# Attention scores of two units in the upper and lower half of TensorE's rows, on odd steps

## The chip, the cores and the metric

The kernel runs on one core of a Trainium2 chip. The metric is device microseconds of the whole program, lower is better. TensorE (PE in the profile) multiplies, VectorE (DVE), ScalarE (ACT) and GpSimd (POOL) work on rows of data, and SyncE (SP) issues most of the transfers. TensorE first loads a stationary operand (PEld) and then streams a moving one past it into PSUM.

## The reference, cut to what matters

Two layers, each an attention and then a mixture of eight experts, over 32 batches of 128 positions with 256 features. The change touches the attentions alone, which have 16 heads of 16 features:

```
q, k, v = layernorm(x) @ Wq, ctx @ Wk, ctx @ Wv    # layer 0 with biases
scores  = einsum('bhqd,bhkd->bhqk', q, k) / 4       # layer 1: minus the causal and the key mask
out     = softmax(scores) @ v                       # 16 heads x 16 features
x       = x + tanh(g) * out                         # layer 0 has W_O in front
```

## The kernel before

**Units.** A unit is four heads of one batch, and there are `NU` = 128 units in each layer (L = 0, 1). Unit i belongs to batch i // 4, and the four units of a batch take heads 0 to 3, 4 to 7, 8 to 11 and 12 to 15. The 256 features lie as two blocks of 128 rows (`m`), so a block holds the heads of two units: the even unit's four heads are rows 0 to 63 and the odd unit's are rows 64 to 127 (`z`). The scores of a unit are one matrix product of the queries (stationary, 128 features x 128 positions) with `KX` (moving, 128 features x 4 heads x 128 keys), in which each head's keys stand in that head's 16 rows and the rest is zero. Each operand is split in a rounded high part and a low rest, and `three` (lines 407 to 411) adds high x high, high x low and low x high. Layer 1 adds the mask with a fourth product (line 488).

**Steps.** Every engine runs through the same list of steps s = -8 to 147, each in its own written order, and they meet at semaphores. Unit i passes so: TensorE makes its scores in step i - 4, into one of three PSUM banks (`SB_[i % 3]`); VectorE takes the row extremes in step i - 3 (line 1094); ScalarE takes the exponentials in step i - 2 (line 698), which frees the bank; TensorE transposes them in step i (line 470), ScalarE copies the transposed weights out (line 705), and TensorE multiplies them with the values in step i + 2 (line 553), each head in 32 columns of the array. When a batch's four units are summed up, ScalarE copies the sums to `OS` (line 691) and TensorE turns them in step 4b + 6 (line 495); VectorE normalises them in the next step (lines 1098 and 1104). The turned weights and sums take turns in two banks (`PTB`).

**Work of a group.** A group is four batches, 16 steps. `grp(s, k)` is true at step k modulo 16. Spread over the 16 steps are the projections for a later group: turned layer norm at steps 6 and 7 (`X0`), queries at 8 and 9 (`Q0`), keys at 0 and 2 (`K0`), values at 10 and 11 (`V0`), and for the router turned rows at 13 and 14 (line 526), logits at 15 (line 534) and ranks at 2 (lines 540 and 541). In layer 0 there is an output projection for each batch too (lines 511 and 517). In layer 0 all these share one PSUM bank (`BK`), and a use waits until the one before it was read (`bank_free`). After a key projection ScalarE takes the high part (line 649 or 651), VectorE the low part (877 or 879, in `dve_rests` of the next step), and SyncE copies a batch's keys into `KX` with eight transfers (`sp_keys`, line 1444).

**Order in a step before.** TensorE: weights of unit s turned, scores of unit s + 4, sums turned, projections, router work, values of unit s - 2. VectorE: extremes of unit s + 3, sums normalised, `dve_rests`, then the rest. ScalarE: sums, exponentials of unit s + 2, turned weights of unit s, then the rest.

Of the kernel before, what the change touches and what calls it, by code (L numbers as in the profile page):

```python
# [11 lines left out]
ALU = mybir.AluOpType  # L12
AX = mybir.AxisListType
# [5 lines left out]
G = 4  # L19
# [106 lines left out]
NU = 4 * B  # L126
FIRST, LAST = -8, 148
X0, Q0, K0, V0 = (6, 7), (8, 9), (0, 2), (10, 11)
# [8 lines left out]
def bat(s, k):  # L137
    b, m = divmod(s - k, 4)
    return b if m == 0 and 0 <= b < B else None


def program(nc, A):
    ctx = ExitStack()
    with ctx:
# [300 lines left out]

        def pe_first(e, w, L):

            if L == 0:
                w.wait_ge(*s_kz[0, 0])
                for n in range(WARM):  # L450
                    e.matmul(PTB[1][:, :], KXR[:, 0:128], KXR[:, 0:512], start=True, stop=True)
            for m in range(2):
                pe_key(e, w, L, 0, m)
            for h in range(2):
                pe_value(e, w, L, 0, h)
            for t in range(2):
                pe_turn(e, w, L, 0, t)
            for m in range(2):
                w.wait_ge(*v_k[L, 0, m])
                pe_query(e, w, L, 0, m)  # L460

        def pe_attention(e, w, L):
            pe_first(e, w, L)
            for s in range(FIRST, LAST):
# [7 lines left out]
                if 0 <= s + 4 < NU:  # L472
                    i = s + 4
                    b, m, z = i // 4, (i // 2) % 2, i % 2
                    g, j, bank = b // G, b % G, SB_[i % 3]
                    w.wait_ge(*v_q[L, g, 1])
                    if i < 2:
                        w.wait_ge(*a_v[L, 0, i])
                    w.wait_ge(*d_k[b % 2][L, b, 7])
                    if i >= 3:  # L480
                        w.wait_ge(*a_p[L, i - 3])
                    js = slice(j * 128, j * 128 + 128)
                    kh, kl = (KX[:, b % 2, p, m, 4 * z:4 * z + 4, :].rearrange("p h k -> p (h k)") for p in range(2))
                    ins = three(e, bank[:, :], (QR[:, g % 2, 0, m, js], QR[:, g % 2, 1, m, js]), (kh, kl), True, L == 0)
                    if L == 1:
                        w.wait_ge(*v_mk[g])
                        w.wait_ge(*s_ir[0])
                        ins = e.matmul(bank[:, :], IR[:, :], MK[:, g % 2, j:j + 1, :].to_broadcast([128, 4, 128]), start=False, stop=True)  # L488
                    ins.then_inc(*m_s(L, i))
                if (b := bat(s, 6)) is not None:  # L490
                    bank = pt_place["o", b]
                    w.wait_ge(*a_o[L, b])
                    turn_free(w, L, "o", b)
                    for n in range(4):
                        ins = e.transpose(bank[:, n * 128:(n + 1) * 128], OS[:, n * 128:(n + 1) * 128], ident)  # L495
                    ins.then_inc(*m_o(L, b))
# [45 lines left out]
                if 0 <= s - 2 < NU:  # L542
# [12 lines left out]
                    ins.then_inc(*m_av(L, i))  # L555

# [528 lines left out]

        def dve_attention(e, w, L):
            dve_first(e, w, L)
            for s in range(FIRST, LAST):
                if 0 <= s + 3 < NU:
                    i = s + 3  # L1090
                    w.wait_ge(*m_s[L, i])
                    if i >= 4:
                        w.wait_ge(*a_p[L, i - 4])
                    e.tensor_reduce(mx[:, i % 4], SB_[i % 3][:, :].rearrange("p (h k) -> p h k", h=4), AX.X, ALU.min).then_inc(*v_mx(L, i))  # L1094
# [14 lines left out]
                dve_rests(e, w, L, s - 1)  # L1109
                for j in range(G):  # L1110
                    if L == 1 and (g := grp(s, -3 + j)) is not None:
                        dve_add_rows(e, w, g * G + j)
# [509 lines left out]
```

## Time and profile before

| | before |
|---|---|
| three runs | 1713.99, 1715.84 and 1717.71 us, median 1715.84 |
| the profiled execution | 1715.62 us, its span 1713.8 us |
| busy: TensorE, weight loads | 1595.4 us, 1406.1 us |
| busy: VectorE, ScalarE, GpSimd | 1199.4, 1233.1, 827.5 us |
| attention of layer 0, steady part | about 60 to 370 us of the span |
| attention of layer 1, steady part | about 940 to 1250 us |

The experts take most of what is left, and the change doesn't touch them. Busy shares are averages over stages, so the steady part of each attention is read by itself. A matmul's duration includes its way through the array: what one costs in a stream is read from the distance of one start to the next, which the chain of waits shows.

### The profile page before, as it was taken

The page shows a single profiled execution, that of the slowest core. Times are in us where ns is not written, and L with a number is a line of the kernel's source. Part 1 is how long each engine was busy: PE and PEld are TensorE (multiplying, and loading weights), DVE is VectorE, ACT ScalarE, POOL GpSimd, SP SyncE. Part 2 cuts the span into 40 slices and gives each one's busy share as a digit, 9 for nine tenths or more (in the row PEclk, how much of TensorE's full clock was granted, in tenths as well). Part 3 has the DMA queues.
Part 4 walks back from the last instruction along what each step waited for, and adds up shares of the span by engine and source line. Part 5 has one row for each costly group of instructions (what it writes and reads, how often), then busy time and mean ns, then how long its engine had stood idle before and what let it go on. Part 6 is the DMA issues. An engine that isn't in the chain of part 4 may idle for free.

```text
span 1713.8 us, 37210 instructions
## 1 busy us (share of the span) xinstructions
PE 1595.4 (93%) x12792; PEld 1406.1 (82%) x12792; DVE 1199.4 (70%) x2843; ACT 1233.1 (72%) x2859; POOL 827.5 (48%) x888
## 2 busy tenths in 40 slices
PE   6999999996899999999995999999994899999996
PEld 4777777774899999999994776776773899999996
DVE  4666777756577777777775778888866666666663
ACT  3887877771688888888872877777782577777774
POOL 3124433434365565656553113333323477777775
PEclk8999999996899999999997999999996999999998
DMA  3222222133877777788762223332231688887883
GB/s 108 50 51 74 72 73 75 51 87 87 246 237 229 227 231 226 229 227 232 225 191 72 76 82 104 98 95 72 90 92 65 204 236 227 225 241 222 229 230 98
DMA packets 208989, 256.57 MB, mean 150 GB/s; under 512 B 29555, under 2 KB 156788, under 8 KB 208800
## 3 DMA queue, kind: packets, MB, share of 16 engines
q1 hardware_dynamic: 186048, 218.22, 43.9%
q0 software_dynamic: 21120, 34.39, 7.8%
q8 instruction: 102, 1.67, 0.4%
q10 hardware_dynamic: 1632, 1.58, 0.3%
q14 instruction: 87, 0.71, 0.1%
HBM read 194.54 MB, written 45.74 MB: 140 GB/s over the span
## 4 chain that ended last, share of the span: by engine, by line
PE 76%; DVE 12%; issue 3%; POOL 3%; DMA 2%; ACT 2%; SPq 1%; POOLq 0%; DVEq 0%; ACTq 0%
PE ps L409 20%; PE ps L411 19%; PE ps L410 19%; PE ps L470 6%; PE ps L553 4%; PE ps L564 2%; DVE mx L1094 2%; POOL xs_scr L1345 1%; PE ps L534 1%; SPq L1444 1%; PE ps L495 1%; PE ps L488 1%; PE ps L526 1%; DVE X L1017 1%; PE ps L424 1%
## 5 line engine op out<-in xcount | busy, mean ns | idle before, releaser
L1217 POOL TENSOR_TENSOR KXR<-U,KXR 128x1024 fp32r<-128x1024 f32 (+1 forms) x156 | 355.4, 2278 | 278.4 <-ACT KXR L750 258.9
L409 PE MATMUL ps<-QR,KXR 128*128 128x256 f32 x1248 | 361.9, 290 | 4.2 <-DVE QR L1221 4.2
L411 PE MATMUL ps<-QR,KXR 128*128 128x256 f32 x1248 | 355.6, 285 | 0.0
L410 PE MATMUL ps<-QR,KXR 128*128 128x256 f32 x1248 | 355.4, 285 | 0.0
L750 ACT ACTIVATE KXR<-U 128x1024 fp32r<-128x1024 f32 (+1 forms) x312 | 287.4, 946 | 75.5 <-PE ps L411 50.4
L698 ACT ACTIVATE U<-ps,mx 128x128 f32<-128x128 f32 x1024 | 294.9, 391 | 26.3 <-DVE mx L1094 26.0
L409 PEld LDWEIGHTS ps<-QR,KXR 128*128 128x128 f32 x1248 | 241.8, 194 | 5.7 <-DVE QR L1221 5.3
L410 PEld LDWEIGHTS ps<-QR,KXR 128*128 128x128 f32 x1248 | 241.8, 194 | 0.0
L411 PEld LDWEIGHTS ps<-QR,KXR 128*128 128x128 f32 x1248 | 241.4, 193 | 0.0
L1094 DVE TENSOR_REDUCE mx<-ps 128x4 f32<-128x512 f32 x256 | 174.9, 685 | 87.2 <-PE ps L411 38.3
L1217 DVE TENSOR_TENSOR KXR<-U,KXR 128x1024 fp32r<-128x1024 f32 (+1 forms) x156 | 176.3, 1168 | 25.7 <-ACT KXR L750 25.5
L1345 POOL DMA_INDIRECT xs_scr<-XR,PI x112 | 109.6, 979 | 142.9 <-DVE PI L1005 113.8
L470 PE MATMUL ps<-cst,U 128*128 128x128 f32 x1024 | 168.4, 287 | 2.7 <-DVE U L1104 2.2
L705 ACT ACTIVATE U<-ps 128x512 f32<-128x512 f32 x256 | 161.8, 632 | 10.8 <-PE ps L470 10.1
L776 ACT ACTIVATE U<-ps,b1s 128x256 f32<-128x256 f32 x312 | 130.1, 471 | 32.5 <-PE ps L411 32.5
L470 PEld LDWEIGHTS ps<-cst,U 128*128 128x128 f32 x1024 | 108.4, 141 | 54.0 <-issue 41.6
L1248 DVE TENSOR_TENSOR PTR<-U,PTR 128x512 fp32r<-128x512 f32 x80 | 100.8, 1295 | 63.2 <-ACT PTR L787 63.2
L409 PE MATMUL ps<-KXR,PTR 128*128 128x256 f32 x480 | 136.3, 284 | 2.4 <-ACT U L765 1.5
L1248 DVE TENSOR_TENSOR WR<-U,WR 128x512 fp32r<-128x512 f32 x76 | 98.0, 1326 | 56.7 <-ACT WR L787 56.7
L410 PE MATMUL ps<-KXR,PTR 128*128 128x256 f32 x480 | 136.0, 283 | 0.0
L411 PE MATMUL ps<-KXR,PTR 128*128 128x256 f32 x480 | 136.0, 283 | 0.0
L409 PE MATMUL ps<-KXR,QR 128*128 128x512 f32 x256 | 122.4, 478 | 14.6 <-ACT U L698 11.5
(204 smaller groups left out, 4042.3 us busy)
## 6 DMA issues: line engine op xcount, KB each, us to landing
U<-in_wpack SPq DMA_DIRECT2D x234, 512.0 KB, 5.0
U<-in_wpack SPq DMA_DIRECT2D x78, 256.0 KB, 4.7
KXR<-U SPq DMA_DIRECT2D x512, 32.0 KB
U<-xs_scr SPq DMA_DIRECT2D x39, 258.0 KB, 4.5
U<-xs_scr SPq DMA_DIRECT2D x39, 257.0 KB, 4.7
U<-in_ctx_t SPq DMA_DIRECT2D x16, 512.0 KB, 5.4
U<-ys_scr SPq DMA_DIRECT2D x32, 256.0 KB, 3.3
XR<-in_L_ffn_b SPq DMA_DIRECT2D x39, 128.0 KB, 4.1
```

What stands on the lines that cost most here:

```text
L409: e.matmul(o, wh, xh, start=first, stop=False)
L410: e.matmul(o, wh, xl, start=False, stop=False)
L411: return e.matmul(o, wl, xh, start=False, stop=done)
L470: ins = e.transpose(bank[:, h * 128:(h + 1) * 128], PB[:, i % 3, h], ident)
L698: ins = e.activation(PB[:, i % 3, h], SB_[i % 3][:, h * 128:(h + 1) * 128], ACT.Exp, bias=mx[:, i % 4, h:h + 1], scale=-1.0)
L705: e.activation(PT[:, i % 3].rearrange("p h k -> p (h k)"), pt_place["p", i][:, :], ACT.Copy).then_inc(*a_pt(L, i))
L750: e.activation(w_cols(L, WH, n), w_raw(L, n), ACT.Copy).then_inc(*a_w[n](L, i))
L776: ins = e.activation(HB[:, r, f], HBK[q][:, z * 256:z * 256 + 256], ACT.Relu, bias=b1s[:, r, f:f + 1])
L1094: e.tensor_reduce(mx[:, i % 4], SB_[i % 3][:, :].rearrange("p (h k) -> p h k", h=4), AX.X, ALU.min).then_inc(*v_mx(L, i))
L1217: e.tensor_tensor(w_cols(L, WL, n), w_raw(L, n), hi, ALU.subtract).then_inc(*l_w[n](L, i))
L1248: ins = e.tensor_tensor(low[:, 2 * q:2 * q + 2], HB[:, i % 2, 2 * q:2 * q + 2], high[:, 2 * q:2 * q + 2], ALU.subtract)
L1345: e.indirect_dma_start(xs_d[L], bass.IndirectOffsetOnAxis(ap=PI[:, g % 2, z, j:j + 1], axis=0), xr(g)[:, z, j, 0:ROWS[L]], None).then_inc( ...
```

## The change

It has four parts.

1. Scores are made on odd steps alone, for units s + 3 and s + 4 together (`pe_scores`). Each of the six products takes 64 of the 128 rows: the even unit's lower half, the odd unit's upper half, in turn, into two banks. In layer 1 the two mask products follow, over all rows.
2. VectorE takes the extremes of unit s + 3 as before on even steps (first in the step), and on odd steps behind `dve_rests` (`dve_least`).
3. TensorE turns the sums at the end of step 4b + 6, behind the values product, and not before the projections.
4. The second key projection of a group moves from step 2 to step 1.

```diff
--- before.py
+++ after.py
@@ -125,7 +125,7 @@
 PARTS = [Part(g, 0, G) for g in range(NG - 1)] + [Part(NG - 1, 0, G - 1), Part(NG - 1, G - 1, G)]
 NU = 4 * B
 FIRST, LAST = -8, 148
-X0, Q0, K0, V0 = (6, 7), (8, 9), (0, 2), (10, 11)
+X0, Q0, K0, V0 = (6, 7), (8, 9), (0, 1), (10, 11)
 
 
 def grp(s, k):
@@ -443,6 +443,31 @@
                                 (WR[:, 2, 0, t], WR[:, 2, 1, t]), t == 0, t == 1)
             ins.then_inc(*m_v(L, g, h))
 
+        def pe_scores(e, w, L, i):
+
+            b, m = i // 4, (i // 2) % 2
+            g, js, banks = b // G, slice(b % G * 128, b % G * 128 + 128), (SB_[i % 3], SB_[(i + 1) % 3])
+            w.wait_ge(*v_q[L, g, 1])
+            if i == 0:
+                for n in range(2):
+                    w.wait_ge(*a_v[L, 0, n])
+            w.wait_ge(*d_k[b % 2][L, b, 7])
+            for n in range(2):
+                if i + n >= 3:
+                    w.wait_ge(*a_p[L, i + n - 3])
+            for q, k in ((0, 0), (0, 1), (1, 0)):
+                for z, bank in enumerate(banks):
+                    hs = slice(64 * z, 64 * z + 64)
+                    ins = e.matmul(bank[:, :], QR[hs, g % 2, q, m, js], KX[hs, b % 2, k, m, 4 * z:4 * z + 4, :].rearrange("p h k -> p (h k)"),
+                                   start=(q, k) == (0, 0), stop=L == 0 and q == 1)
+                    if L == 0 and q == 1:
+                        ins.then_inc(*m_s(L, i + z))
+            if L == 1:
+                w.wait_ge(*v_mk[g])
+                w.wait_ge(*s_ir[0])
+                for z, bank in enumerate(banks):
+                    e.matmul(bank[:, :], IR[:, :], MK[:, g % 2, b % G:b % G + 1, :].to_broadcast([128, 4, 128]), start=False, stop=True).then_inc(*m_s(L, i + z))
+
         def pe_first(e, w, L):
 
             if L == 0:
@@ -469,31 +494,8 @@
                     for h in range(4):
                         ins = e.transpose(bank[:, h * 128:(h + 1) * 128], PB[:, i % 3, h], ident)
                     ins.then_inc(*m_t(L, i))
-                if 0 <= s + 4 < NU:
-                    i = s + 4
-                    b, m, z = i // 4, (i // 2) % 2, i % 2
-                    g, j, bank = b // G, b % G, SB_[i % 3]
-                    w.wait_ge(*v_q[L, g, 1])
-                    if i < 2:
-                        w.wait_ge(*a_v[L, 0, i])
-                    w.wait_ge(*d_k[b % 2][L, b, 7])
-                    if i >= 3:
-                        w.wait_ge(*a_p[L, i - 3])
-                    js = slice(j * 128, j * 128 + 128)
-                    kh, kl = (KX[:, b % 2, p, m, 4 * z:4 * z + 4, :].rearrange("p h k -> p (h k)") for p in range(2))
-                    ins = three(e, bank[:, :], (QR[:, g % 2, 0, m, js], QR[:, g % 2, 1, m, js]), (kh, kl), True, L == 0)
-                    if L == 1:
-                        w.wait_ge(*v_mk[g])
-                        w.wait_ge(*s_ir[0])
-                        ins = e.matmul(bank[:, :], IR[:, :], MK[:, g % 2, j:j + 1, :].to_broadcast([128, 4, 128]), start=False, stop=True)
-                    ins.then_inc(*m_s(L, i))
-                if (b := bat(s, 6)) is not None:
-                    bank = pt_place["o", b]
-                    w.wait_ge(*a_o[L, b])
-                    turn_free(w, L, "o", b)
-                    for n in range(4):
-                        ins = e.transpose(bank[:, n * 128:(n + 1) * 128], OS[:, n * 128:(n + 1) * 128], ident)
-                    ins.then_inc(*m_o(L, b))
+                if s % 2 and 0 <= s + 3 < NU:
+                    pe_scores(e, w, L, s + 3)
                 for name, at, project in (("xt", X0, pe_turn), ("q", Q0, pe_query), ("k", K0, pe_key), ("v", V0, pe_value)):
                     for n in range(2):
                         if (g := grp(s, at[n])) is not None:
@@ -553,6 +555,13 @@
                         ins = e.matmul(OB[32 * h:32 * h + 32, (i % 4) * 128:(i % 4) * 128 + 128], VA[:, v, j % 2, hh * 17:hh * 17 + 32],
                                        PT[:, i % 3, h], start=True, stop=True)
                     ins.then_inc(*m_av(L, i))
+                if (b := bat(s, 6)) is not None:
+                    bank = pt_place["o", b]
+                    w.wait_ge(*a_o[L, b])
+                    turn_free(w, L, "o", b)
+                    for n in range(4):
+                        ins = e.transpose(bank[:, n * 128:(n + 1) * 128], OS[:, n * 128:(n + 1) * 128], ident)
+                    ins.then_inc(*m_o(L, b))
 
         def pe_turn_x(e, w, L, i):
             bank = XB[i % 2]
@@ -1083,15 +1092,17 @@
                 e.tensor_scalar(IR[:, :], ident, NEG_L, None, ALU.mult).then_inc(*s_ir(0))
             e.memset(CR[:, 0], 0.0).then_inc(*v_c.up())
 
+        def dve_least(e, w, L, i):
+            w.wait_ge(*m_s[L, i])
+            if i >= 4:
+                w.wait_ge(*a_p[L, i - 4])
+            e.tensor_reduce(mx[:, i % 4], SB_[i % 3][:, :].rearrange("p (h k) -> p h k", h=4), AX.X, ALU.min).then_inc(*v_mx(L, i))
+
         def dve_attention(e, w, L):
             dve_first(e, w, L)
             for s in range(FIRST, LAST):
-                if 0 <= s + 3 < NU:
-                    i = s + 3
-                    w.wait_ge(*m_s[L, i])
-                    if i >= 4:
-                        w.wait_ge(*a_p[L, i - 4])
-                    e.tensor_reduce(mx[:, i % 4], SB_[i % 3][:, :].rearrange("p (h k) -> p h k", h=4), AX.X, ALU.min).then_inc(*v_mx(L, i))
+                if s % 2 == 0 and 0 <= s + 3 < NU:
+                    dve_least(e, w, L, s + 3)
                 if (b := bat(s, 7)) is not None:
                     w.wait_ge(*m_o[L, b])
                     o = pt_place["o", b][:, :].rearrange("p (h d) -> p h d", d=32)
@@ -1107,6 +1118,8 @@
                         w.wait_ge(*v_on[1, b])
                         e.scalar_tensor_tensor(X[:, b], ON[:, b % 2], th[:, 1:2], X[:, b], ALU.mult, ALU.add).then_inc(*v_xup(1, b))
                 dve_rests(e, w, L, s - 1)
+                if s % 2 and 0 <= s + 3 < NU:
+                    dve_least(e, w, L, s + 3)
                 for j in range(G):
                     if L == 1 and (g := grp(s, -3 + j)) is not None:
                         dve_add_rows(e, w, g * G + j)
```

## Rows read from the trace of the kernel before

**Rows 1.** The windows view, steady part of each attention: busy us of each engine.

```profile
core 0: us, PE busy (x) PEld busy (x) DVE busy (x) ACT busy (x) POOL busy (x), PEclk, DMA share, GB/s
60.00:370.00 310.00, 305.10 (x2587) 235.19 (x2585) 214.36 (x654) 252.10 (x709) 111.69 (x239) 1.00 0.25 65
940.00:1250.00 310.00, 297.35 (x2342) 220.53 (x2341) 252.02 (x727) 231.82 (x661) 93.93 (x220) 1.00 0.31 88
```

**Rows 2.** The chain of waits in layer 0: start us, us, what.

```profile
188.26 0.44 PE ps L424 x4
188.70 0.35 PE ps L553 x8
189.05 0.59 PE ps L470 x4
189.64 0.23 PE ps L409
189.87 0.24 PE ps L410
190.11 0.23 PE ps L411
...
208.33 0.12 PE ps L409
...
211.12 1.68 PE ps L534 x16
```

**Rows 3.** The timeline of layer 0: start us, us, what, idle before and its cause.

```profile
199.93 0.48 PE L409 MATMUL ps<-KXR,QR 128*128 128x512 f32 x1
200.01 0.19 PEld L410 LDWEIGHTS ps<-KXR,QR 128*128 128x128 f32 x1
...
202.59 0.42 PEld L470 LDWEIGHTS ps<-cst,U 128*128 128x128 f32 x4 [0.20 <-issue]
...
204.09 0.16 PEld L553 LDWEIGHTS ps<-U,VA 128*32 128x32 f32 x8 [0.17 <-issue]
```

**Rows 4.** The windows view, one group of 16 steps of layer 0.

```profile
174.40:219.60 45.20, 44.22 (x375) 34.33 (x374) 32.18 (x103) 36.28 (x102) 18.18 (x39) 1.00 0.27 71
```

**Rows 5.** The windows view, one group of 16 steps of layer 1.

```profile
1133.60:1180.30 46.70, 44.39 (x357) 33.06 (x356) 38.78 (x122) 34.35 (x98) 15.85 (x37) 1.00 0.35 97
```

**Rows 6.** Groups of instructions in layer 0: busy us, mean ns, idle before, releaser.

```profile
L698 ACT ACTIVATE U<-ps,mx 128x128 f32<-128x128 f32 x512 | 147.3, 391 | 4.4 <-DVE mx L1094 4.4
L1094 DVE TENSOR_REDUCE mx<-ps 128x4 f32<-128x512 f32 x128 | 87.5, 687 | 48.5 <-PE ps L411 38.3 <-ACT U L698 9.5
...
L705 ACT ACTIVATE U<-ps 128x512 f32<-128x512 f32 x128 | 80.4, 628 | 9.3 <-PE ps L470 8.8
...
L691 ACT ACTIVATE OS<-ps 128x512 f32<-128x512 f32 x32 | 19.3, 605 | 2.7 <-PE ps L553 1.4
```

**Rows 7.** The windows view, slices of 10 us, layer 0.

```profile
220.00:230.00 10.00, 9.02 (x77) 6.50 (x77) 9.12 (x35) 7.25 (x22) 4.63 (x15) 1.00 0.11 24
...
250.00:260.00 10.00, 10.00 (x88) 8.35 (x87) 6.26 (x21) 9.55 (x25) 3.06 (x2) 1.00 0.13 28
...
400.00:410.00 10.00, 5.75 (x23) 4.54 (x22) 6.42 (x44) 2.64 (x7) 2.34 (x6) 0.50 0.10 35
```

**Rows 8.** The windows view, slices of 10 us, layer 1.

```profile
1080.00:1090.00 10.00, 9.55 (x79) 6.81 (x78) 9.17 (x48) 5.96 (x19) 3.11 (x13) 1.00 0.09 19
1090.00:1100.00 10.00, 8.13 (x57) 5.85 (x58) 9.54 (x26) 7.86 (x23) 5.89 (x6) 1.00 0.29 87
```

**Rows 9.** Who waited for whom, TensorE, layer 0: us, times, longest us.

```profile
PE ps L540 <- DVE U L877: 4.9, 5, 1.0
```

**Rows 10.** Who waited for whom, VectorE, layer 0.

```profile
DVE mx L1094 <- PE ps L411: 33.2, 51, 1.5
```

**Rows 11.** The chain of waits in layer 1.

```profile
1022.51 0.23 PE ps L411
1022.74 0.24 PE ps L488
1023.00 0.69 DVE mx L1094
1023.70 0.18 DVE rec L1098
1023.89 0.44 DVE U L1104
1024.35 0.48 DVE X L1108
1024.84 2.59 DVE X L1017
```

**Rows 12.** The timeline of SyncE's queue, layer 0.

```profile
188.34 5.09 SPq L1444 DMA_DIRECT2D KXR<-U  x8
```

## The prediction

> **What bounds the kernel now.** I read the windows of the two steady attentions first. In layer 0 TensorE is busy 305 of 310 us, ScalarE 252 and VectorE 214; in layer 1 it is 297, 232 and 252, all at a granted clock of 1.00 [rows 1]. The chain of waits says the same: in layer 0 it stays on TensorE for tens of microseconds. A step without extra work is 0.35 us for the values product, 0.59 for the turned weights and 3 x 0.233 = 0.70 for the scores, together 1.64 us [rows 2]. ScalarE isn't far behind. Per unit it spends 147.3 / 128 = 1.15 us on exponentials and 80.4 / 128 = 0.63 on the copy, 1.78 in all, which is more than the bare step of TensorE [rows 6]. The units add up to less than TensorE's total only because TensorE has the projections too: a group of 16 steps in layer 0 takes 45.2 us, with TensorE busy 44.2, ScalarE 36.3 and VectorE 32.2 [rows 4]. Inside a group the bound changes: in one slice of 10 us ScalarE is busy 9.55, in another VectorE is busy 9.12 and TensorE idles 0.98 [rows 7]. In layer 1 a group takes 46.7 us with VectorE busy 38.8 [rows 5], for two slices in a row it is at 9.2 and 9.5 while TensorE idles up to 1.9 [rows 8], and the chain passes through it there [rows 11].
>
> **What the change saves on TensorE.** Before, a pair of units costs 6 x 0.233 = 1.40 us of scores [rows 2]. Each product streams 512 columns and keeps the full array, though half of its rows are multiplied with zeros. After, there are still six products of 512 columns, but neighbours sit in different rows. The trace has no such pair, so I bound it. Above: they run one after the other, 1.40 us. Below: the two halves run at once, 3 x 0.233 = 0.70. In between stands the load of the stationary operand, which each product has for itself: sixteen products of 8 columns take 1.68 us, so 0.105 us for a load of 128 columns [rows 2]. Six loads one after another, with the last stream behind them, are 5 x 0.105 + 0.233 = 0.76 us. Do products in different parts of the array overlap at all? The values product does this in columns: eight instructions of 128 columns in 0.35 us, 0.044 each [rows 2], where 128 columns at the rate of the scores (0.233 / 4) would be 0.058 each. That speaks for overlap, though it is weak evidence for rows. I take 0.76, a saving of 0.64 us a pair.
>
> **What it costs on TensorE.** The turned weights take 0.59 us behind the values product, but the same four transposes (lines 424 and 495) take 0.44 behind full products, and the first load behind a change between 32 columns and the full array starts 0.20 or 0.17 us late with nothing to wait for [rows 2, 3]. So a change in how the array is divided costs about 0.15 us. The new scores bring one change on the way in. On the way out there is another one if full-array work follows; with the values product next, that change was there already. Of the eight odd steps of a group in layer 0, six have such work behind the scores (1, 7, 9, 11, 13, 15): 8 + 6 = 14 changes, 2.1 us. In layer 1 the mask product always follows: 16 changes, 2.4 us. From both sides: a change into halves may cost nothing, or 0.20 plus a load, 0.30. The Trainium skill (TensorEngine Tiling (Array Packing), Key Properties) says that changing the tiling mode drains TensorE, while moving to another tile of the same mode does not. The rows agree where they can, with 0.15 us for columns; by the rule the price is there for rows as well, and the sum is the one used here.
>
> Net, a group saves 8 x 0.64 - 2.1 = 3.0 us in layer 0 and 8 x 0.64 - 2.4 = 2.7 in layer 1. If all of it lay on the path, 8 groups each would give 24 + 22 = 46 us.
>
> **How much of it is on the path.** In layer 0 a pair of bare steps is bound by ScalarE already: 2 x 1.78 = 3.56 us, and the copy of sums (19.3 / 32 = 0.60 a batch) comes on top, against TensorE's 3.3 us [rows 2, 6]. Steps 3 to 5 and 12 therefore give nothing back, and in steps 0 to 2 VectorE is nearly full [rows 7]. The projections of steps 6 to 11 and the router's work of 13 and 15 are TensorE's. I count two thirds: 8 x 3.0 x 2/3 = 16 us. In layer 1 about 20 of 46.7 us of a group are VectorE's [rows 5, 8], and the change takes nothing from it; I count half: 8 x 2.7 / 2 = 11 us.
>
> **The key projection.** In layer 0 the rank product (line 540) shares its bank with the key projection and waited for the low part of the keys of the same step, which VectorE makes one step later: 5 waits, 4.9 us [rows 9]. With the projection in step 1, VectorE makes that part in step 2, so this wait goes. What is late next is VectorE itself, full in that slice [rows 7]. I count 3 us. The other side: the second key projection now waits for the low part of the first, one step apart instead of two. Queued behind it on TensorE are the values product of that step and the next turned weights, and ScalarE's copy waits for those. Between the two projections lie 0.35 + 0.59 + 0.91 = 1.85 us of TensorE work; the read-out takes one pass of ScalarE and one of VectorE at about 0.7 each (the extremes of 128 x 512 take 0.687 [rows 6]), so it is just hidden. If not, it costs up to 0.5 us a group, 4 us. In layer 1 there are two banks, so nothing changes.
>
> **The moved pieces.** The scores of the even unit come a step later, and with them its extremes, which stand behind `dve_rests`. The cover is the time until ScalarE wants them in the next step. Now VectorE waits in each odd step for TensorE's scores of that same step, with the statistics and the router's small operations queued behind, and ScalarE waits for those extremes. VectorE's wait at this place is 33.2 us in 51 times already [rows 10], and idle time there has cost nothing. The sums are turned 4 x 0.11 = 0.44 us as before, later in the step by the values product and the extra work (up to 0.35 + 0.7 us); normalising them must be done two transposes later. Between lie 0.59 + 0.91 + 0.35 us, against 0.18 + 0.44 for lines 1098 and 1104 [rows 11]: hidden, nothing. The keys' eight transfers wait for the same odd unit's scores, made in the same step as before, and are issued in 5.1 us [rows 12], and their reader comes one step later, so SyncE's queue has more room. GpSimd's queue isn't touched.
>
> **Sum.** 16 + 11 + 3 = 30 us. The profiled execution took 1715.6 us with a span of 1713.8, 1.8 us around it, and the median is 1715.8, so the two agree: 1715.8 - 30 = 1686 us. With only this case in view, its own range is 1664 (all 46 us and the 4.9 of the wait) to 1704 (0.30 us for each change, which adds 30 x 8 x 0.15 = 36 us on TensorE, of which half counts, 18).
>
> **Rivals.**
>
> A. The halves don't overlap. A pair keeps 1.40 us, and the changes are pure cost: 8 x (2.1 + 2.4) = 36 us. TensorE is the bound, so nearly all of it counts: 36 - 3 = 33, 1749 us. For it: no row shows overlap in rows. Against it: the 0.044 us of the values product [rows 2].
>
> B. A load waits for the stream that still runs in its own half. Each half then goes load, stream, load, stream, 3 x (0.105 + 0.233) = 1.01 us, with the other half 0.1 behind: 1.12 a pair. It saves 8 x 0.28 = 2.2 us a group against 2.1 to 2.4 for the changes, so the time is 1713 to 1717. Against it: the load of line 410 starts at 200.01, while the stream of line 409 over the same rows runs from 199.93 for 0.48 us [rows 3]. The Trainium skill (TensorE: Matmul & The Clock Gate, Part 3) says that a load overlaps a running matmul only when the row group differs. This row of the profile does not agree, and that keeps the chance small.
>
> C. A loop through three engines takes the place of TensorE. The pair of scores at step s needs the exponentials of unit s + 1; then come the extremes of s + 3, its exponentials, and the next pair. That is 0.15 + 0.76 + 0.69 + 1.15 with three handovers of 0.1, 3.1 us (3.3 with the mask), under ScalarE's 3.56. It is the bound once 0.5 us of queueing is added: sums to normalise and rests stand before the extremes, the last copy and a projection's read-out before the exponentials. It loses against before when it costs 30 / 128 = 0.24 us a pair above the forecast. At 0.5 us a pair it costs 64 - 30 = 34 us more than before, 1750; I put the case at 1720 to 1755, its middle at 1735. For it: three banks give only one unit of slack when two are filled at once. Against it: in steps with projections ScalarE has slack.
>
> D. ScalarE and VectorE hide all of it, so only the rank wait shows: 1713 us. For it: ScalarE's 9.55 and VectorE's 9.12 [rows 7]. Against it: in layer 0 TensorE is the chain nearly everywhere.
>
> E. The changes cost little and the rest follows: 8 x 2 x 8 x 0.64 = 82 us at the most, two thirds of it 55: about 1655.
>
> A fall of the granted clock would be visible at once: in a slice with TensorE at 5.8 of 10 us it was 0.50, 1.2 GHz, and with 8.1 busy it stayed 1.00, 2.4 GHz [rows 7, 8]. After the change TensorE is still over 8, so I give that no case.
>
> **How the numbers follow.** Chances: forecast 0.58, A 0.10, B 0.05, C 0.13, D 0.06, E 0.08. Within 0.2% (3.4 us, about what a measurement of this kernel can tell from no change) lie B and D: 0.08, with a bit of each on the fast side. Faster is forecast and E and that bit, 0.69; slower A and C, 0.23. To hold 8 in 10 the range takes half of E, the forecast, B, D and most of C: 1658 to 1738.
>
> **What would show it.** Right: in the chain the six products of a pair together take about 0.76 us, the first load of them starts 0.15 to 0.2 us late, a group of layer 0 takes about 43 us and one of layer 1 about 45.3, the wait of line 540 is gone. Wrong: 0.23 us between starts of neighbours (A), 0.37 us between passes (B), or waits of the scores or the turned weights for ScalarE, and of ScalarE for the extremes, that grow by more than 0.24 us a pair (C).

## The result, and the profile after

The changed kernel takes 1758.05 us in the median of four runs (1752.97 to 1762.94), against 1715.93 before: a ratio of 1.0245 (95% interval 1.0207 to 1.0284), 42 us slower where 30 us faster was forecast. The profiled execution took 1754.1 us, with a span of 1752.3.

The loss lies in the two attentions. The windows view from the first to the last exponential of each layer, first before, then after (span of the window, then busy us of TensorE, its loads, VectorE, ScalarE and GpSimd, then the granted clock):

```profile
29.40:377.70 348.30, 333.79 (x2785) 255.24 (x2784) 234.23 (x699) 277.22 (x783) 120.67 (x266) 0.99 0.26 70
940.60:1291.20 350.60, 334.88 (x2674) 247.48 (x2672) 278.15 (x821) 264.64 (x759) 104.71 (x243) 1.00 0.31 89
```

```profile
29.30:401.10 371.80, 326.72 (x2785) 229.87 (x2786) 233.29 (x699) 275.71 (x783) 120.62 (x266) 0.95 0.24 65
961.50:1329.30 367.80, 328.31 (x2673) 219.01 (x2674) 276.15 (x821) 264.85 (x759) 105.98 (x243) 0.97 0.30 85
```

23.5 us are lost in layer 0 and 17.2 in layer 1. TensorE's work did get less (busy 7 us less in each layer, although its clock is lower). Its idle time grew from 15 to 45 us in layer 0 and from 16 to 40 in layer 1. VectorE and ScalarE do what they did.

TensorE's own terms came out at the forecast size. The chain of waits of the changed kernel, layer 0, which answers to [rows 2]:

```profile
213.91 0.90 PE ps L461 x6
214.81 0.59 PE ps L528 x4
215.40 0.36 PE ps L555 x8
215.75 0.58 PE ps L495 x4
```

And the timeline of its loads, which answers to [rows 3]:

```profile
213.84 0.54 PEld L461 LDWEIGHTS ps<-KXR,QR 64*128 64x128 f32 x6 [0.17 <-issue]
214.74 0.42 PEld L528 LDWEIGHTS ps<-cst,XR 128*128 128x128 f32 x4 [0.36 <-issue]
```

Six products of 64 rows take 0.90 us with the change on the way in (0.76 + 0.15 = 0.91 was forecast), and the four transposes behind them 0.59 in place of 0.44, the change on the way out. So the halves do run at once. The timeline of the same six products, at three moments within it, shows how:

```profile
213.84 0.51 PE L461 MATMUL ps<-KXR,QR 64*128 64x512 f32 x2
214.17 0.40 PE L461 MATMUL ps<-KXR,QR 64*128 64x512 f32 x2
214.40 0.41 PE L461 MATMUL ps<-KXR,QR 64*128 64x512 f32 x2
```

Two products, one in each half, start together, three times. The starts lie 0.33 and 0.23 us apart, and 0.23 is what one full product takes [rows 2]. The prediction had the six loads one after another and so came to 0.76; what runs is three passes of 0.23 us, 0.70, with about 0.2 us on the way in. The sum is the same, its parts are not.

What came on top are waits. Who waited for whom, TensorE and then VectorE, layer 0 of the changed kernel, which answer to [rows 9, 10]:

```profile
PE ps L424 <- DVE U L1047: 16.3, 6, 3.1
PE ps L542 <- DVE U L886: 4.4, 5, 0.9
PE ps L409 <- DVE QR L876: 4.4, 7, 0.6
PE ps L409 <- DVE PTR L870: 3.2, 6, 0.6
```

```profile
DVE rec L1109 <- PE ps L563: 61.8, 29, 3.4
DVE mx L1099 <- PE ps L461: 12.5, 33, 1.0
```

ScalarE waited for the extremes too, before and then after:

```profile
ACT U L698 <- DVE mx L1094: 2.5, 1, 2.5
```

```profile
ACT U L707 <- DVE mx L1099: 16.9, 20, 1.1
```

About once a group TensorE stands before the turned layer norm (line 424), up to 3.1 us, because VectorE's norm (line 1047, 1038 before) is late. The rank product (542) waits as it did. The projections now wait about 0.6 us each time for the read-out of the shared bank (rests 870 and 876). VectorE waits 61.8 us for the sums, where before it waited once, 2.2 us, and less for scores. And the granted clock falls behind the long wait. Windows, two slices of 10 us and a part of the second one, right behind the wait of 3.1 us that ends at 191.46:

```profile
180.00:190.00 10.00, 7.47 (x76) 4.93 (x74) 8.25 (x33) 7.59 (x24) 3.55 (x14) 1.00 0.12 25
190.00:200.00 10.00, 8.02 (x54) 6.04 (x55) 5.89 (x14) 5.87 (x17) 7.98 (x9) 0.83 0.51 159
192.00:195.00 3.00, 3.00 (x20) 2.39 (x20) 0.00 (x0) 1.86 (x6) 2.53 (x3) 0.50 0.78 282
```

In the kernel before all 62 slices of 10 us from 60 to 370 us and from 980 to 1290 us are at 1.00; in the changed kernel eleven of them are at 0.83 to 0.85, and two more at 0.98 and 0.99.

A group of layer 0 takes 48.8 us (181.53 to 230.31, from one rank product to the next) in place of 45.2 [rows 4]; in layer 1 three groups in a row take 48.5 to 50.0 us in place of 46.9. How VectorE's full stretch got longer can be read from its timeline, from the first key rest (line 877, then 886) to the second pair of norms. Before:

```profile
214.48 0.69 DVE L1094 TENSOR_REDUCE mx<-ps 128x4 f32<-128x512 f32 x1
...
216.56 0.75 DVE L877 SCALAR_TENSOR_TENSOR U<-ps,bqk,U 128x512 fp32r<-128x512 f32 x1 [1.39 <-ACT U L649]
...
229.24 0.73 DVE L1038 TENSOR_SCALAR U<-X,mv,rs 128x256 f32<-128x256 f32 x2
```

After:

```profile
224.90 0.75 DVE L886 SCALAR_TENSOR_TENSOR U<-ps,bqk,U 128x512 fp32r<-128x512 f32 x1 [1.52 <-ACT U L658]
...
226.22 0.69 DVE L1099 TENSOR_REDUCE mx<-ps 128x4 f32<-128x512 f32 x1 [0.25 <-PE ps L461]
...
231.90 0.26 DVE L1109 RECIPROCAL rec<-ps 128x16 f32<-128x16 f32 x1 [1.18 <-PE ps L563]
...
239.38 0.72 DVE L1047 TENSOR_SCALAR U<-X,mv,rs 128x256 f32<-128x256 f32 x2
```

12.7 us became 14.5. Before, one reduction ran ahead of the key rest, in time that was idle otherwise (1.39 us were still idle behind it); now its scores don't exist yet at that point, it stands inside the stretch (0.69 + 0.25 us), and 1.18 us go in waiting for the sums. TensorE meanwhile has less to do between rank product and layer norm, so it arrives early and stands.

### The profile page after: what moved, and what is told of

Read it like the earlier page. It is cut to its first block, busy times and chain, and to the rows that moved or that the text cites. A ratio compares the mean times of both kernels' runs of the same rounds, so it can differ in the third digit from the quotient of the medians.

```text
span 1752.3 us, 37272 instructions
## 1 busy us (share of the span) xinstructions
PE 1578.5 (90%) x12792; PEld 1348.8 (77%) x12792; DVE 1196.1 (68%) x2843; ACT 1232.3 (70%) x2859; POOL 828.3 (47%) x888
## 3 DMA queue, kind: packets, MB, share of 16 engines
q10 hardware_dynamic: 1632, 1.58, 0.3%
## 4 chain that ended last, share of the span: by engine, by line
PE 67%; DVE 15%; issue 6%; POOL 4%; DMA 3%; ACT 3%; SPq 1%; POOLq 0%; DVEq 0%; ACTq 0%
PE ps L409 17%; PE ps L411 16%; PE ps L410 16%; PE ps L461 4%; PE ps L495 4%; DVE mx L1099 3%; PE ps L555 2%; POOL xs_scr L1358 2%; PE ps L573 2%; PE ps L563 2%; DMA U<-xs_scr 1%; PE ps L469 1%; PE ps L536 1%; DVE U L1047 1%; DVE PTR L870 1%
## 5 line engine op out<-in xcount | busy, mean ns | idle before, releaser
L495 PEld LDWEIGHTS ps<-cst,U 128*128 128x128 f32 x1024 | 114.0, 144 | 55.7 <-issue 39.5
L461 PE MATMUL ps<-KXR,QR 64*128 64x512 f32 x768 | 127.1, 436 | 10.8 <-ACT U L707 7.8
```

The lines of the kernel that those rows point to most:

```text
L461: ins = e.matmul(bank[:, :], QR[hs, g % 2, q, m, js], KX[hs, b % 2, k, m, 4 * z:4 * z + 4, :].rearrange("p h k -> p (h k)"), start=(q, k) ...
L495: ins = e.transpose(bank[:, h * 128:(h + 1) * 128], PB[:, i % 3, h], ident)
```

## The experiments

Two theories stood at the start. **T**: the sums, turned late, block VectorE at the head of its queue, and all else follows from that. **P**: pairing the scores takes away cover, whatever the sums do. Others were formed on the way.

Eighteen runs were made in five sets, each set on a chip of its own. The chips are of two kinds: on two of them the kernel before takes 1716 to 1717 us, as in the result above, and on three it takes 1760 to 1764 (called the faster and the slower kind below). Ratios are to the kernel before in the same set, and differences in us are taken within one set, or between sets on chips of one kind where it says so. Windows of a layer come from one profiled execution each.

**First set (before: 1763 us, slower kind).** The times expected here were written for a chip on which the kernel before takes 1716 us, so each is read by its distance from the kernel before. What is undone, in short:

```diff
 # e1: the sums turned before the projections, as before
-                if (b := bat(s, 6)) is not None:      # behind the values product
+                if (b := bat(s, 6)) is not None:      # ahead of the projections
 # e3: all score products over full rows
-  QR[hs, g % 2, q, m, js], KX[hs, b % 2, k, m, ...]
+  QR[:, g % 2, q, m, js],  KX[:, b % 2, k, m, ...]
 # e4: the kernel before, sums turned behind the values product, and
-X0, Q0, K0, V0 = (6, 7), (8, 9), (0, 2), (10, 11)
+X0, Q0, K0, V0 = (6, 7), (8, 9), (0, 1), (10, 11)
 # e5: e1, and K0 back to (0, 2)
```

> The changed kernel with one thing undone: the sums are turned before the projections again, as in the kernel before. Theory T (the late turn blocks VectorE at the head of its queue, 61.8 us of its waiting in layer 0, and that makes the layer norm and all behind it late): about 30 to 45 us come back, 1700 to 1725 us, VectorE's wait for the sums falls below 15 us and line 424 waits less than 5 us in layer 0. Theory P (pairing the scores on odd steps takes the cover from the read-outs of the shared bank and from VectorE's work, whatever the sums do): at most 10 us come back, 1745 to 1758 us.

Measured: 1784.5 us, 1.0134 (1.0108 to 1.0161), 21.6 us above before: between the two theories.

> The changed kernel with each of the six score products over all 128 rows, one after another; order and placement as changed. It tells what the halves themselves are worth. If TensorE were still the bound everywhere, a pair would cost 1.40 us in place of 0.76 and save two changes of 0.15 to 0.2 us: 0.3 us a pair, 128 pairs, 35 to 40 us slower than the changed kernel, 1790 to 1800 us. If waits on VectorE and ScalarE are the bound (both theories), about half of it: 1770 to 1780 us.

Measured: 1813.4 us, 1.0289 (1.0260 to 1.0319), 50.5 us above before, less than either case expected. The changed kernel isn't in this set; the fourth set has both.

> The kernel before with two parts of the change alone: the sums turned at the end of the step, and the second key projection in step 1 (the late turn needs it). Theory T: slower by 20 to 40 us than before, 1736 to 1756 us, with VectorE waiting 30 us or more in layer 0 for the sums. Theory P: within 5 us of before.

Measured: 1767.8 us, 1.0032 (1.0012 to 1.0052), 4.8 us above before as P has it, though VectorE does wait 41 us for the sums in layer 0.

> The changed kernel with the turn of the sums and the key projection where they stood before: pairs of scores in halves of the rows and the placement of the extremes alone. Theory T: faster than before, 1690 to 1710 us. Theory P: still slower than before, 1740 to 1758 us.

Measured: 1793.4 us, 1.0173 (1.0139 to 1.0206), 30.4 us above before, as P has it.

Against the 1.0245 of the changed kernel, e1 looked like a gain of 19 us and so like T; the fourth set takes that back. Within this set P holds: with the old turn and the old key projection the paired order is still slower than before (e5). And pairing is dear by itself: e3 and e4 both have full rows, the late turn and the key projection in step 1, and differ in the pairing with its placement of the extremes (which is free when the scores aren't paired, e12). It costs 1813.4 - 1767.8 = 45.7 us. Moving the key projection is worth 8.9 us (e5 against e1). With that, the late turn isn't free either: e4 has both and is 4.8 us slower than before, so by an estimate the late turn costs 12 to 14 us in the old order (4.8 and the 7.4 of e6 or the 8.9).

**Second set (before: 1717 us, faster kind).** The fill goes ahead of the wait for the layer norm, into the bank that is overwritten next:

```diff
 # e7
+            if g and t == 0:
+                for n in range(10):
+                    e.matmul(bank[:, :], WR[:, 0, 0, 0, 0:128], WR[:, 0, 0]..., start=True, stop=True)
             w.wait_ge(*v_ln1[L, g])
 # e8
-X0, Q0, K0, V0 = (6, 7), (8, 9), (0, 1), (10, 11)
+X0, Q0, K0, V0 = (7, 8), (9, 10), (0, 1), (11, 12)
 # e6: the kernel before with K0 = (0, 1)
```

> The changed kernel, unaltered, to have its ratio and its trace on the chip that the other runs of this set share. Both theories: ratio to before 1.02 to 1.03.

Measured: 1764.4 us, 1.0296 (1.0270 to 1.0322).

> The kernel before with the second key projection in step 1 in place of step 2, nothing else. By the prediction 3 us faster (the wait of 4.9 us for the rank product goes); by the rival the projection's new wait for the shared bank costs up to 4 us. Ratio 0.998 to 1.002.

Measured: 1709.4 us, 0.9963 (0.9951 to 0.9974): 7.4 us faster, more than the 3 us forecast. Of the parts that were run alone on the kernel before it is the one that helps, and this kernel is faster than both. The changed kernel lies 55.0 us above it in this set.

> The changed kernel with ten idle products of 512 columns (their results are overwritten) ahead of TensorE's wait for the layer norm of each later group, 14 places, 2.3 us each at full clock where the wait is 2 to 3 us. Theory C (the lower granted clock behind these waits is a cost of its own): the stretches at 0.50 right behind the turned layer norm vanish, 14 times up to 1.7 us, 10 to 20 us faster than the changed kernel. Theory W (only the waits count, the clock costs nothing because TensorE isn't the bound there): within 4 us of the changed kernel, or slower.

Measured: 1749.6 us, 1.0200 (1.0183 to 1.0217), 14.8 us faster than the changed kernel by its side. Windows of the changed kernel again and of the fill, the slice behind the layer norm:

```profile
240.00:250.00 10.00, 7.72 (x53) 5.63 (x54) 6.36 (x15) 5.86 (x17) 7.98 (x9) 0.83 0.48 154
```

```profile
240.00:250.00 10.00, 8.64 (x73) 5.98 (x74) 6.21 (x15) 7.37 (x22) 7.60 (x9) 1.00 0.54 164
```

Fourteen times ten useless products make the kernel faster, because TensorE works on behind the wait at 2.4 and not at 1.2 GHz. Of the 62 slices of 10 us named above, twelve lie below 1.00 in the changed kernel of this set and one with the fill. Theory C holds.

> The changed kernel with the turned layer norm, the query and the value projections one step later (7 to 12 in place of 6 to 11). VectorE gets one step more for the layer norm, and the score pair of step 7 comes before it. Theory S (in steps 0 to 5 VectorE is the bound and TensorE's savings there turn into the wait for the layer norm): that wait falls from 16 us in layer 0 and 10 in layer 1 to under 5 each, and the time falls by 15 to 30 us. Rival: the wait moves to the query projection or the scores of step 13, and the time stays within 6 us.

Measured: 1742.7 us, 1.0161 (1.0134 to 1.0189), 21.7 us faster than the changed kernel. TensorE no longer waits for the layer norm there; the row that is left for line 424 is the shared bank:

```profile
PE ps L424 <- DVE PTR L870: 2.4, 5, 0.5
```

So about half of the loss sat in that one wait. The other half stayed, and part of the wait moved, as the rival has it: TensorE now waits for the read-out of the output projection:

```profile
PE ps L409 <- DVE OT L900: 9.7, 6, 1.8
```

The granted clock falls behind such a wait too (at 190.5 us, behind 1.77 us of waiting). Of the same 62 slices 14 are below 1.00, the lowest of them:

```profile
140.00:150.00 10.00, 8.82 (x59) 5.80 (x59) 6.21 (x15) 6.35 (x18) 7.90 (x8) 0.66 0.50 153
```

**Third set (before: 1716 us, faster kind).**

```diff
 # e12: the kernel before, K0 = (0, 1), extremes by parity, scores unpaired
-                if 0 <= s + 3 < NU:                  # first in the step
+                if s % 2 == 0 and 0 <= s + 3 < NU:   # first in the step
+                ...
+                dve_rests(e, w, L, s - 1)
+                if s % 2 and 0 <= s + 3 < NU:        # behind the rests
 # e14: the changed kernel, sums normalised (bat(s, 7)) behind the extremes
 # e16: the changed kernel;  e17: the kernel before with K0 = (0, 1)
-            uses, nb = uses_bk(L), L + 1
+            uses, nb = uses_bk(L), 1
```

> The kernel before with the second key projection in step 1 and VectorE's extremes placed by step parity (behind dve_rests on odd steps); scores and sums as before. The key alone was 0.9963 of before. Theory V (the extremes behind the rests lengthen VectorE's full stretch in steps 0 to 5 by one reduction, 0.69 us a group): 5 to 11 us slower than the key alone, 1.000 to 1.003. Rival (the placement is free): 0.996.

Measured: 1711.7 us, 0.9975 (0.9962 to 0.9987), 2.3 us above the key alone on another chip of this kind and not told apart from it. Unpaired, the placement is free.

> The changed kernel with VectorE's normalising of the sums moved behind dve_rests and the extremes of the same step, so that the late turn no longer stops VectorE's queue. Theory T (the late turn costs by VectorE's idle time at the head of its queue): VectorE's wait for the sums falls from 62 us in layer 0 to under 15, and 10 to 20 us come back, 1.013 to 1.019. Rival (VectorE would have been idle there anyway): within 4 us of the changed kernel, 1.023 to 1.028.

Measured: 1779.2 us, 1.0365 (1.0335 to 1.0396): 12 to 21 us worse than the changed kernel by its two ratios on other chips of this kind. VectorE's wait moved from the sums to the extremes, and TensorE's turned weights now wait for the bank of the sums:

```profile
DVE mx L1099 <- PE ps L461: 62.9, 43, 2.7
```

```profile
PE ps L495 <- DVE U L1118: 12.2, 15, 1.1
```

Taking the sums from the head of VectorE's queue gave nothing back: on odd steps it waits for the pair of scores, whatever stands first. The run doesn't clear the late turn of all cost, since the edit made a wait of its own.

> The changed kernel with one shared bank for projections and router in layer 1 too, as layer 0 has. Theory B (without scores on even steps nothing covers the read-out of a shared bank): 3 to 4 waits of 0.6 us a group more, 10 to 20 us slower than the changed kernel, and more than the same edit costs the kernel before. Rival: under 5 us.

Measured: 1784.2 us, 1.0408 (1.0381 to 1.0434), 19.8 us above the changed kernel of the second set.

> The kernel before with the key projection in step 1 and one shared bank in layer 1. Theory B: under 5 us slower than the key alone (0.9963), so 0.996 to 1.000. Rival (one bank costs both orders the same): as much as it costs the changed kernel.

Measured: 1720.6 us, 1.0025 (1.0013 to 1.0037). The window of layer 1 from first to last exponential goes from 351.6 to 359.4 us in the old order, and from 369.8 to 394.5 in the changed one (e6 to e17, e10 to e16, two sets on chips of one kind). That would be 7.8 against 24.7 us, but the profiled executions of e17 and e10 were the fastest of theirs, each 5.7 us below its median. By the medians one bank costs the old order 11.2 us (e17 against e6) and the paired order 19.8. So it costs the paired order about twice as much. Theory B holds in direction; the size in the paired order was as expected, and in the old order it was larger.

**Fourth set (before: 1764 us, slower kind).** e24, e21 and e20 are the changed kernel, e3 and e1 again; e19 is e16 with a fourth score bank in layer 1:

```diff
-            (SB_[i % 3], SB_[(i + 1) % 3])
+            (SBL[L][i % (3 + L)], SBL[L][(i + 1) % (3 + L)])   # SBL = (PS[0:3], PS[0:3] + PS[7:8])
```

> The changed kernel, unaltered, as the reference of this set of four. All theories: 1.024 to 1.030 of before.

Measured: 1790.4 us, 1.0157 (1.0135 to 1.0179). Below the range: on this chip the change costs 27 us, not 42 to 48.

> The changed kernel with all score products over full rows, once more, beside the changed kernel on one chip. By the busy time of TensorE (352 against 327 us in layer 0) the halves save 25 us a layer. If TensorE bound the paired order, the changed kernel would be 45 to 50 us faster than this. Theory W (the paired order is bound by waits and part of what the halves save turns into waits and a lower clock): 5 to 20 us.

Measured: 1815.6 us, 1.0279 (1.0232 to 1.0326): the halves are worth 25 us by the medians and 21 to 22 by the ratios, a little more than theory W has and half of what a bound by TensorE would give. Windows from first to last exponential, changed kernel and then full rows:

```profile
28.10:412.10 384.00, 331.15 (x2784) 232.53 (x2785) 233.94 (x701) 276.08 (x783) 121.54 (x268) 0.94 0.23 63
973.30:1367.30 394.00, 343.89 (x2675) 228.23 (x2676) 276.97 (x822) 265.79 (x760) 106.57 (x244) 0.93 0.28 79
```

```profile
29.60:424.00 394.40, 350.70 (x2792) 267.45 (x2794) 235.14 (x701) 277.30 (x784) 121.69 (x268) 0.96 0.23 61
985.00:1390.20 405.20, 357.60 (x2675) 263.08 (x2676) 276.46 (x822) 265.85 (x760) 106.64 (x244) 0.96 0.27 77
```

TensorE is busy 33 us less in both layers together, and they end 22 us earlier.

> The changed kernel with the sums turned before the projections again, once more, on one chip with the changed kernel. From the first run, 1.0134 on another chip: 15 to 25 us faster than the changed kernel. Rival (that difference was the chip's): within 5 us.

Measured: 1785.6 us, 1.0129 (1.0107 to 1.0151), 4.8 us faster, with intervals that overlap. The large effect that e1 seemed to show was the chip's. As the main cause theory T has fallen, on this kind of chip; on the faster kind the turn wasn't put back.

> The changed kernel with four score banks in layer 1 in place of three; the bank comes from the projections, which share one there as in the run that gave 1.0408 and 394 us for the exponentials of layer 1. Theory L (the loop from exponentials over scores and extremes, which three banks close, binds the paired order): layer 1 falls by 10 to 25 us against that run, 1.027 to 1.035. Rival (banks are no bound): layer 1 stays at 390 to 398 us, 1.039 to 1.042.

Measured: 1820.6 us, 1.0348 (1.0317 to 1.0380). The total is near the expected one, but by the chip alone; layer 1 decides. It takes 422.8 us against 394.0 of the changed kernel by its side, 28.8 more, and one bank without a fourth score bank had cost 24.7 by the windows on the faster kind. A fourth bank gives nothing in layer 1, and theory L has fallen there. Layer 0 had no such run.

**Fifth set (before: 1760 us, slower kind).** The layer norm of groups 1 to 7 moves to GpSimd, `if (g := grp(s, 3 + n)) is not None: dve_norm(...)` in its loop.

> The changed kernel with the layer norm of the later groups (four operations of 0.4 us a group, 14 groups) made by GpSimd in steps 3 and 4 in place of VectorE in steps 4 and 5. Theory S (VectorE's full stretch eats what TensorE saves): TensorE's wait for the layer norm, 16 us in layer 0 and 10 to 14 in layer 1, falls below 5 each, and 20 to 35 us come back: 1.004 to 1.014 of before on a chip where the changed kernel is 1.0245 to 1.0296. Rival (the loss is spread over all steps): under 10 us, above 1.019.

Measured: 1795.9 us, 1.0195 (1.0168 to 1.0223). On this kind of chip the changed kernel was at 1.0157 (e24), so nothing came back.

> The kernel before with the key projection in step 1 and the same move of the layer norm to GpSimd. Theory S: TensorE hardly waits for the layer norm in this order, so 0 to 8 us against the key alone (0.9963), 0.992 to 0.997. Rival (VectorE's work is worth the same in either order): it gains as much as the changed kernel does.

Measured: 1762.1 us, 1.0003 (0.9987 to 1.0018), above the range of theory S and no gain either. The pair doesn't decide: GpSimd is as late in layer 0 of e25 as VectorE was, so the wait was not taken away, only renamed:

```profile
PE ps L424 <- POOL U L1047: 15.6, 6, 2.7
```

## Why the prediction was wrong, point by point

- **TensorE's price of a pair: right in size, in part by luck.** 0.89 to 0.94 us with the way in at the full clock, against 0.91 (behind the long waits, at the lower clock, up to 1.58), and about 0.15 on the way out. But 0.76 was worked out from six loads one after another, and the loads start in pairs as the products do: the lower bound of 0.70 holds, and the way in takes 0.2 in place of 0.15. Rival A (a start each 0.23 us) and rival B (0.37 us between passes) are out.
- **"How much of it is on the path": nearly right for the halves alone.** 16 + 11 = 27 us were forecast, and against the same order in full rows 25 us were measured (on the slower kind of chip). The shares of two thirds and a half were reasoned for the old order, so the agreement is partly luck. And the forecast compared with the wrong kernel: that gain is against the paired order, and not against the order before.
- **"The moved pieces": this step failed.** It took the paired order as free, "idle time there has cost nothing", and gave it no term in the sum. Pairing in full rows costs 45.7 us (e3 against e4, slower kind of chip). The prediction summed the work of each engine and asked for each moved piece whether one wait would grow. What it missed is that the scores of the even steps were cover and buffer. With them gone, TensorE reaches the next projection before the shared bank is read (e16 and e17: 20 against 11 us for one bank in layer 1), VectorE can't take a reduction early in its idle time (seen in its timeline, not tested by a run), and TensorE arrives early at the end of VectorE's full stretch and stands before the layer norm (e8: one step more gives back 21.7 us). The late turn, "hidden, nothing", costs about 12 to 14 us in the old order by the estimate above, and 4.8 us in the paired one (e20), which is at the edge of what the runs tell apart.
- **"A fall of the granted clock ... I give that no case": wrong.** The argument went by the busy share of 10 us. In the slice of 190 to 200 us above, behind a wait of 3.1 us, TensorE is still 8 of 10 busy and the mean clock is 0.83; what the clock costs behind this wait is 14.8 us (e7). How far this overlaps with what e8 gives back isn't shown: in e8 the wait is gone, but 14 slices are at a lower clock there against 12 in e10. It also hides the saving: the prediction counted 24 and 22 us less work for TensorE, and its busy time fell by 7.1 and 6.6. By an estimate from busy time and mean clock of each window above, the work at full clock fell by 20 and 16 us.
- **The key projection: right in sign, too small.** 7.4 us in place of 3. Its group in layer 0 takes 44.0 us in place of 45.2, and TensorE's rank product no longer waits for the keys there. In the changed kernel that wait, said to go, stays (4.4 us), since VectorE is later there, and in layer 1 the rank product has a new one of 4.7 us in six times (line 542 for line 942), where none was listed before.
- **Small sums.** By their own terms rival E comes to 1658 us and not 1655 (1715.8 - 55 - 3), and the lower end of the case's range to 1665 and not 1664. Nothing rests on either.
- **Rival C: the right side, near the right size, and only part of its mechanism.** It gave 1720 to 1755 with 1735 as its middle, for a loop from exponentials over scores to extremes. One link of the loop did get slower: in layer 0 ScalarE waits 16.9 us for extremes in place of 2.5, about the 0.24 us a pair that was named as the sign; in layer 1 it is 22.6 in place of 21.5. The link that three banks close did not: TensorE's scores wait for exponentials as long as before (5.7 us in layer 1 both times, none listed in layer 0), and in layer 1 a fourth bank doesn't help.

Against the kernel before, on the slower kind of chip: pairing +45.7, halves -25, late turn and key together +4.8 (e4 against before), which gives +25.5, and +26.8 was measured. The first and the last of these terms are e3 against before, split at e4, so this agreement says only that e3 came out the same twice (50.5 and 52.0 us above before). On the faster kind, where the result was measured, pairing in full rows wasn't run. There the changed kernel is 55.0 us slower than the key move alone (e10 against e6), which holds pairing, halves and late turn together.

Why the same change costs 15 to 21 us more on the faster kind stays open. The traces do differ: on the slower kind ScalarE and TensorE stand idle at times without a wait on another engine or a transfer that the profile shows. In layer 0 from 60 to 400 us ScalarE does so for 12.4 us in e24, and for 12.4 to 25.2 in all ten runs on the slower kind, against at most 0.3 in the ten traces of the faster one; TensorE for 2.8 to 11.0 against at most 0.6. The largest row of e24:

```profile
ACT U L714 <- issue: 5.2, 3, 1.9
```

What these stops are, and whether they hide part of what the change costs, isn't shown.

How the 45.7 us split between shared bank, VectorE's stretch and clock stays open too: the runs show each of the three, but they overlap, and no run takes all of them away.

## What to carry to other kernels

Doing the same work in fewer, larger lumps costs cover: list for each shared bank and each nearly full engine what ran between a write and its read-out, and price the order with the old work in it before pricing the work that is saved. When an engine is made faster ahead of a stretch that another engine bounds, the saving turns into a wait, and here TensorE paid for such a wait twice, since the granted clock behind it was lower (e7: 14.8 us for 14 waits). Try the small parts of a bundle alone: here one line of it was worth 7 us, and the rest lost 55 (e6 and e10).

## What the runs showed of the hardware

- Two products of 64 rows in different halves, each with a stationary operand of its own and f32r data, overlap fully: they start together, and three such pairs start 0.33 and 0.23 us apart where full rows take 0.23 each. Six of 64 rows take 0.90 us with the way in, six of full rows 1.40. Their loads start in pairs as well.
- The change of how the array is divided costs about the same for rows as for columns, 0.15 to 0.20 us, both ways. The Trainium skill (TensorEngine Tiling (Array Packing), Key Properties) says that such a change drains TensorE; the rows of lines 461 (first load 0.17 us late) and 528 (0.59 us in place of 0.44) fit that, and put this price on it.
- Useless products in waits of up to 3.1 us made the kernel 14.8 us faster over 14 waits, about 1 us each. Without them the granted clock fell behind such a wait: in the changed kernel it is at 0.50 from 192.0 to 195.0 us with TensorE busy throughout, behind the wait that ends at 191.46, and at 1.00 again from 195.5. In e8 it also fell behind a wait of 1.8 us.
- The same kernel before took 1716 to 1717 us on some chips and 1760 to 1764 on others, and the ratio of the changed kernel was 1.0245 and 1.0296 on the first kind, 1.0157 on the second. A comparison over sets misled by 14 us here (e1). The traces of the slower kind have 12.4 to 25.2 us in which ScalarE stands idle without a cause that the profile shows, in 340 us of layer 0, where the faster kind has at most 0.3.
